# Splitting the down weights and the first row tile's values while the last up products run, in two feed-forward stages of a fused eight-stage network

## What is computed

```python
# L1_ffn: weights (w - zero) * scale, zero and scale per group of 128 rows
gate = jax.nn.silu(jnp.dot(x, gate_proj))
up = jnp.dot(x, up_proj)
return jnp.dot(gate * up, down_proj)
# L3_ffn, the last block: weights w_int * scale, one scale for each matrix
x_mid = jax.nn.silu(x_gate) * x_up
x_out = _qlinear(x_mid, w_down, scale_down)
```

## Time and profile before

| | |
|---|---|
| time, median of 3 runs | 1424.2 us (1423.32 to 1424.61) |
| the profiled execution | 1424.28 us, span 1422.4 us |
| TensorE matmuls busy | 1288.9 us, 91% |
| VectorE busy | 733.9 us, 52% |
| ScalarE busy | 429.2 us, 30% |
| mean granted TensorE clock | 0.949 |
| L376 (up products) in L1 and L3 | 1152 matmuls, 264.4 us |
| L393 (down products) in L1 and L3 | 600 matmuls, 141.7 us |

### The profile page before, as it was taken

One profiled execution on the slowest core, in us unless ns is written; L12 is line 12 of the kernel. 1 busy time (PEld: TensorE's weight loads), 2 busy tenths in 40 slices (PEclk: granted clock), 3 DMA queues, 4 the chain that ended last, 5 costly groups with the idle time before them and its releaser, 6 DMA issues. The chain is left out here.

```text
span 1422.4 us, 14508 instructions
## 1 busy us (share of the span) xinstructions
PE 1288.9 (91%) x5416; PEld 847.6 (60%) x5418; DVE 733.9 (52%) x1283; ACT 429.2 (30%) x718; POOL 162.6 (11%) x211
## 2 busy tenths in 40 slices
PE   7999999699799998983887989989999998799998
PEld 4787666344477787773665434445454443488876
DVE  5322432475666555422756755977776731433264
ACT  2122211211311114210122221156656656221141
POOL 0000000000194100001111250000010124000000
PEclk9999999799899999996889898989999999899999
DMA  8110000830255530003000010000000000112001
GB/s 317 45 44 0 0 0 0 332 148 0 82 202 198 221 139 0 1 23 139 1 1 0 1 45 0 1 1 2 2 2 2 2 3 1 45 67 83 5 23 38
DMA packets 18075, 78.88 MB, mean 55 GB/s; under 512 B 2945, under 2 KB 3585, under 8 KB 15842
## 3 DMA queue, kind: packets, MB, share of 16 engines
q1 hardware_dynamic: 18018, 78.13, 14.9%
HBM read 75.76 MB, written 2.10 MB: 55 GB/s over the span
## 5 line engine op out<-in xcount | busy, mean ns | idle before, releaser
L376 PE MATMUL psum<-L_ffn_x,L_ffn_w_up 128*128 128x512 f32 x1152 | 264.4, 391 | 2.9 <-DVE L_ffn_hidden L505 2.9
L376 PEld LDWEIGHTS psum<-L_ffn_x,L_ffn_w_up 128*128 128x128 f32 x1152 | 217.0, 189 | 50.1 <-DVE L_ffn_hidden L505 4.8
L1814 DVE TENSOR_REDUCE mqa_top<-psum 128x1 f32<-128x512 f32 (+3 forms) x304 | 186.0, 655 | 58.1 <-PE psum L1640 37.7
L1733 ACT ACTIVATE mqa_prob<-psum 128x512 f32<-128x512 f32 x288 | 159.8, 601 | 86.0 <-PE psum L1658 84.9
L393 PE MATMUL psum<-L_ffn_wd,L_ffn_part_h 128*128 128x512 f32 x600 | 141.7, 397 | 7.0 <-DVE L_ffn_wd L301 7.0
L1658 PE MATMUL psum<-mqa_stack,mqa_keys 100*128 100x512 f32 x288 | 133.0, 476 | 4.8 <-DMA mqa_stack<-mqa_rows 3.5
L393 PEld LDWEIGHTS psum<-L_ffn_wd,L_ffn_part_h 128*128 128x128 f32 x600 | 114.3, 192 | 31.7 <-DVE L_ffn_part_h L292 7.8
L1629 PE MATMUL psum<-mqa_keys,mqa_stack 96*128 96x512 f32 (+1 forms) x256 | 108.3, 445 | 1.9 <-DVE mqa_top L1814 1.0
L376 PE MATMUL psum<-L_attn_x,L_attn_w_up 128*128 128x512 f32 x456 | 105.4, 394 | 3.9 <-DVE L_attn_hidden L505 3.9
L376 PEld LDWEIGHTS psum<-L_attn_x,L_attn_w_up 128*128 128x128 f32 x456 | 86.7, 190 | 22.5 <-issue 4.3
L1658 PEld LDWEIGHTS psum<-mqa_stack,mqa_keys 100*128 100x128 f32 x288 | 55.3, 196 | 72.0 <-ACT mqa_prob L1733 62.6
(11 more groups left out here) (246 smaller groups left out, 1698.2 us busy)
## 6 DMA issues: line engine op xcount, KB each, us to landing
L_ffn_stage<-in_L_w SPq DMA_DIRECT2D x25, 768.0 KB, 6.3
L_ffn_z_int<-in_L_z SPq DMA_DIRECT2D x14, 768.0 KB, 4.4
L_ffn_s_all<-in_L_s SPq DMA_DIRECT2D x14, 768.0 KB, 6.2
lora_wo<-in_L_wo SPq DMA_DIRECT2D x8, 1024.0 KB, 8.7
L_attn_stage<-in_L_w SPq DMA_DIRECT2D x10, 512.0 KB, 3.7
L_attn_w_down<-in_L_down SPq DMA_DIRECT2D x1, 2560.0 KB, 24.3
x_feat<-in_x_feat SPq DMA_DIRECT2D x2, 1024.0 KB, 7.0
x_tok<-in_x_tok SPq DMA_DIRECT2D x1, 2048.0 KB, 18.7
```

The costliest lines, as they stand in the source:

```text
L376: ins = nc.tensor.matmul(bank[half][:, :], w_up[:, slot, w_part, at:at + P], x[:, x_part, k, half * HALF:(half + 1) * HALF], start=k == 0 ...
L1733: nc.scalar.activation(prob[:, n % PROBS, :], score_bank[n % 3], ACT.Exp, scale=SCALE)\
L1814: nc.vector.tensor_reduce(top[:, i % 2, lo // HALF, heads[0]:heads[-1] + 1], max_bank[n % 3][:, 0:len(heads) * width] .rearrange("p (h k) ...
```

## The change

Stage L0 keeps its code (`early == 0`). In L3 all down weights (`early = tiles`), and in L1 four of the fourteen (`early = 4`), are split while up products still run.

- **L3.** `wd` moves to memory of its own, and `w_down` shrinks to two slots. In each tile, VectorE now makes the float down weights ahead of the up weights, behind a wait for its own earlier splits; ScalarE casts `wd(0, f)` behind the silu of tile f, and VectorE makes `wd(1, f)` behind its multiplications.
- **L1.** `wd` is made of four pieces that lie where the up phase's buffers end: two tiles in the place of the zeros and scales (free once the last tile's weights are made), two in w_up's slot 0 (free once tile 12's products are done), then eight in x and two in slot 1 (free once all up products are done). The first four are split while tile 13's products run, the other ten behind them.
- **Both.** The last tile's silu and product are taken one half at a time. Behind half 0, both groups' values of row tile 0 are split; row tiles 0 to 3 lie in half 0. The other splits come behind half 1.

The diff, cut:

```diff
+        if zeros is not None:
+            assert (tiles - 1) % 2 == 1
+            part_h = sb("part_h", [P, 2, 2, per, P], F32R)
+            in_front = (front_size - part_size) // (2 * DIM)
+            in_x, in_slot = 2 * KC * TOK // (2 * DIM), 2 * up_width // (2 * DIM)
...
+            places = ([wd_front[:, i, :, :] for i in range(in_front)]
+                      + [wd_slots[:, i, :, :] for i in range(in_slot)]
+                      + [wd_x[:, i, :, :] for i in range(in_x)]
+                      + [wd_slots[:, in_slot + i, :, :] for i in range(in_slot)])
+            early = in_front + in_slot
...
+        elif quantised:
+            early = tiles
...
-        def split_w_down(engine, g, part):
-            for f in groups[g]:
-                if part == 0:
-                    nc.scalar.copy(wd[:, 0, f, :], w_down[:, f, :]).then_inc(wd_hi, 1)
-                else:
-                    engine.wait_ge(wd_hi, base["wd_hi"] + f + 1)
-                    nc.vector.tensor_tensor(wd[:, 1, f, :], w_down[:, f, :], wd[:, 0, f, :].bitcast(F32),
-                                            ALU.subtract).then_inc(wd_lo, 1)
+        def split_w_down(engine, f, part, slot=None):
+            src = w_down[:, f if slot is None else slot, :]
+            if part == 0:
+                nc.scalar.copy(wd(0, f), src).then_inc(wd_hi, 1)
+            else:
+                engine.wait_ge(wd_hi, base["wd_hi"] + f + 1)
+                nc.vector.tensor_tensor(wd(1, f), src, wd(0, f).bitcast(F32),
+                                        ALU.subtract).then_inc(wd_lo, 1)
...
                 def tile(f, slot, first):
                     silu(f, first and slot == 0)
+                    if early == tiles:
+                        split_w_down(act, f, 0, slot)
                     split_w_up(f + 2, slot, False)
...
+                    act.wait_ge(w_lo, base["w_lo"] + tiles)
+                    if early == tiles:
+                        for f in range(tiles - 2, tiles):
+                            split_w_down(act, f, 0, f % 2)
+                    else:
+                        for f in range(in_front):
+                            split_w_down(act, f, 0)
+                        act.wait_ge(up_done, base["up_done"] + 2 * tiles - 2)
+                        for f in range(in_front, early):
+                            split_w_down(act, f, 0)
+                    silu(tiles - 1, halves=(0,))
+                    act.wait_ge(product, base["product"] + 2 * tiles - 1)
+                    for g in range(2):
+                        split_h(act, 0, g, 0)
+                    silu(tiles - 1, halves=(1,))
+                    act.wait_ge(up_done, base["up_done"] + 2 * tiles)
+                    for f in range(early, tiles):
+                        split_w_down(act, f, 0)
+                    act.wait_ge(product, base["product"] + 2 * tiles)
...
                     elif quantised:
                         dve.wait_ge(loaded[slot], base["loaded"][slot] + 8 * (f - slot) + 16)
+                        if not first:
+                            dve.wait_ge(wd_lo, base["wd_lo"] + f - 1)
+                        nc.vector.tensor_scalar(w_down[:, slot, :], w_int[:, slot, up_width:width], sc[:, 2:3], None,
+                                                ALU.mult)
...
-                multiply(tiles - 1)
-                for g in range(2):
-                    split_h(dve, 0, g, 1)
-                    split_w_down(dve, g, 1)
+                if early == 0:
...
+                else:
+                    for f in range(tiles - 2 if early == tiles else 0, early):
+                        split_w_down(dve, f, 1, f % 2 if early == tiles else None)
+                    multiply(tiles - 1, halves=(0,))
+                    for g in range(2):
+                        split_h(dve, 0, g, 1)
+                    multiply(tiles - 1, halves=(1,))
+                    for f in range(early, tiles):
+                        split_w_down(dve, f, 1)
```

More of the change, by code:

```diff
@@ L418, in split_w_up, with silu @@
                     nc.scalar.copy(w_up[:, slot, 0, :], stage[:, slot, 0:up_width]).then_inc(w_hi, 1)
-                def silu(f, fresh=False):
-                    for half in range(2):
+                def silu(f, fresh=False, halves=(0, 1)):
+                    for half in halves:
                         act.wait_ge(gate_done, base["gate_done"] + 2 * f + half + 1)
@@ L438, in _ @@
                 silu(tiles - 2)
-                silu(tiles - 1)
-                act.wait_ge(product, base["product"] + 2 * tiles)
-                if not quantised:
+                if early == 0:
+                    silu(tiles - 1)
+                    act.wait_ge(product, base["product"] + 2 * tiles)
                     act.wait_ge(down_loaded, 16)
+                    for g in range(2):
+                        split_h(act, 0, g, 0)
+                        for f in groups[g]:
+                            split_w_down(act, f, 0)
[4 more added lines that the diff above has]
+                            split_w_down(act, f, 0, f % 2)
+                    else:
+                        for f in range(in_front):
[6 more added lines that the diff above has]
+                    for g in range(2):
+                        split_h(act, 0, g, 0)
+                    silu(tiles - 1, halves=(1,))
+                    act.wait_ge(up_done, base["up_done"] + 2 * tiles)
+                    for f in range(early, tiles):
+                        split_w_down(act, f, 0)
+                    act.wait_ge(product, base["product"] + 2 * tiles)
                 if table is not None:
                     act.wait_ge(table.half_ready, 1)
-                for g in range(2):
-                    split_h(act, 0, g, 0)
-                    split_w_down(act, g, 0)
                 split_h(act, 1, 0, 0)
@@ L492, in split_w_up @@
                         ins.then_inc(dequantised, 1)
-                        nc.vector.tensor_scalar(w_down[:, f, :], w_int[:, slot, up_width:width], sc[:, 2:3], None,
-                                                ALU.mult)
                     if first and slot == 0:
@@ L499, in split_w_up, with multiply @@
                                             w_up[:, slot, 0, :].bitcast(F32), ALU.subtract).then_inc(w_lo, 1)
-                def multiply(f):
-                    for half in range(2):
+                def multiply(f, halves=(0, 1)):
+                    for half in halves:
                         dve.wait_ge(gated, base["gated"] + 2 * f + half + 1)
@@ L509, in tile @@
                     multiply(f)
+                    if early == tiles:
+                        split_w_down(dve, f, 1, slot)
                     split_w_up(f + 2, slot, False)
@@ L518, in _ @@
                 multiply(tiles - 2)
-                multiply(tiles - 1)
-                for g in range(2):
-                    split_h(dve, 0, g, 1)
-                    split_w_down(dve, g, 1)
+                if early == 0:
+                    multiply(tiles - 1)
+                    for g in range(2):
+                        split_h(dve, 0, g, 1)
+                        for f in groups[g]:
+                            split_w_down(dve, f, 1)
+                else:
+                    for f in range(tiles - 2 if early == tiles else 0, early):
+                        split_w_down(dve, f, 1, f % 2 if early == tiles else None)
+                    multiply(tiles - 1, halves=(0,))
+                    for g in range(2):
+                        split_h(dve, 0, g, 1)
+                    multiply(tiles - 1, halves=(1,))
+                    for f in range(early, tiles):
+                        split_w_down(dve, f, 1)
                 split_h(dve, 1, 0, 1)
```

29 lines of the change are left out of this document (23 added, 6 removed).

## The result

| | before | changed |
|---|---|---|
| median | 1424.05 us (1421.98 to 1424.61, 6 runs) | 1414.93 us (1412.49 to 1417.74, 6 runs) |
| profiled execution | 1424.28 us, span 1422.4 | 1412.49 us, span 1410.5 |
| ratio | | 0.9939, 95% interval 0.9927 to 0.995 |

The change makes the kernel 9.1 us faster by the medians, and the interval of the ratio (7.1 to 10.4 us) is clear of zero. A second series on another chip gave the changed kernel 1414.23 us and before 1422.69, ratio 0.9937 (0.9924 to 0.9951).

A forecast was written before the change was run, and what follows sets the result against it. TensorE was taken to bound the kernel except in the holes; gains of 5.4 us in L1 and 5.16 in L3, together 10.56 off 1424.28, gave 1413.7 us, range 1411.4 to 1416.8 (8 in 10: 1411.2 to 1417.4).

The forecast's parts named there:

- The holes: TensorE's idle time ahead of the down products, 3.64 us in L1 and 3.40 in L3, would close to 0 to 0.3.
- T: The end of L1's last up product, put at 539.87 us, from which the readiness of weights and values was counted.
- The falls of the clock: Behind each hole in L1 and L3, TensorE's slow stretch would go, worth 1.6 us each.
- the drops stay: Rival: in L1 and L3 only the holes close and the clock still falls, giving 1416.9 us; chance 0.11.
- L3's loop: The work added to each L3 tile lengthens VectorE's chain from 3.82 to 5.0 us but costs nothing.
- The slower outcome: Rival: the added work in L3's loop makes up weights late, 1.5 us a tile, ending slower; chance 0.03.
- The next stage: The stage behind L1 starts once L1's last row tile is done, so L1's 5.4 us is handed on.
- Matmuls reading `wd` from other places are the same matmuls: Moving the down weights' buffer was taken to leave the down products unchanged, at no cost.
- the term for L3: L3's forecast gain: 3.40 idle, 0.16 lost at the hole and 1.6 of slow clock, 5.16 us.
- The allowance: 2 us to either side for run spread and the clock in stages behind L1, widening 1413.4 to 1414.8.

The follow-up runs named there:

- e7_fill4: The kernel before, with four useless float32 products added behind the last up product in L1 and in L3; 1421.21 us, ratio 0.9979.
- e1_l1_only: The changed kernel with stage L3 run as before, so only L1 is changed; 1418.91 us, ratio 0.9959.
- e2_l3_only: The changed kernel with stage L1 run as before, so only L3 is changed; 1420.55 us, ratio 0.9976.
- e6_pause: The changed kernel, with L3's down products made to wait for the stage's last product; 1416.31 us, ratio 0.9939.
- e8_parts: The changed kernel, but no weight split early in L1 and L3's values split behind the last product; 1420.72 us, ratio 0.9975.

## Why the prediction was right, and its one wrong step

The forecast was 1413.7 us and the median is 1414.93. The mechanism is the forecast one, point by point, but for one step:

- **The holes** close in both stages, as worked out: no idle time at the first down product. L1's values end at 538.15 for 538.4 forecast, 0.12 us of which is that all of L1 lies earlier in this execution (last multiplication at 539.79 for 539.91). Its fifth weight is ready at 541.07, 1.39 us behind the end of the last up product at 539.68, for T + 1.4. (The prediction put T at 539.87; by the earlier trace rows it is 543.44 - 3.64 = 539.80. No sum of it hangs on these 0.07 us.)
- **The falls of the clock** go with them. This was a reading of the trace before; `e7_fill4` shows it apart from all else, 3.0 us (1.7 to 4.3) for 3.2. Of the rivals, "the drops stay" is out. The size of a fall, 1.6 us, is that of one execution; `e1_l1_only` had one that cost 0.9 us more. How often the unprofiled runs of the kernel before had their falls, no row tells.
- **L3's loop** costs nothing. One tile of the changed kernel, VectorE's chain from product to product:

```profile
1245.82 0.69 DVE L564 TENSOR_TENSOR L_ffn_hidden<-L_ffn_gate,psum 128x512 f32<-128x512 f32 x1 [4.75 <-PE psum L411]
1246.43 0.68 DVE L336 TENSOR_TENSOR L_ffn_wd<-L_ffn_w_down,L_ffn_wd 128x512 fp32r<-128x512 f32 x1
1247.22 0.49 DVE L547 TENSOR_SCALAR L_ffn_w_down<-L_ffn_stage,L_ffn_sc 128x512 f32<-128x512 int32 x1
...
1249.62 1.23 DVE L557 TENSOR_TENSOR L_ffn_w_up<-L_ffn_stage,L_ffn_w_up 128x1024 fp32r<-128x1024 f32 x1 [1.12 <-ACT L_ffn_w_up L453]
...
1251.37 0.69 DVE L564 TENSOR_TENSOR L_ffn_hidden<-L_ffn_gate,psum 128x512 f32 x1 [0.53 <-PE psum L411]
```

  It is 1249.62 + 1.23 - 1245.82 = 5.03 us long (5.0 forecast; 3.82 in the earlier trace rows), and VectorE still idles 0.53 us ahead of the next product (0.5 forecast). The 504 up products take 114.25 us, as in the earlier trace rows. The slower outcome is out by a wide margin.
- **The next stage** hands L1's gain on: 5.6 us at its first transfer (5.4 forecast).
- **The wrong step** is the sentence "Matmuls reading `wd` from other places are the same matmuls". They are not. In L3 they stood 0.0067 us wider apart, 1.76 us in all, and the term for L3 is 3.5 in place of 5.16. With it the sum is 5.4 + 3.4 = 8.8, against 9.1 measured. I costed the move of a buffer at nothing, and the trace before could show no price: every stretch that I had read as 0.227 had its operands a multiple of 512 bytes apart, which a profile, without addresses, doesn't tell. The verdict on the time doesn't hang on it: 1.76 us more is 1415.5, inside the range.
- **The allowance** of 2 us for other stages' clock was needed: the median lies 0.1 us above the 1413.4 to 1414.8 that the prediction gave for one execution without it, and the changed kernel's runs spread over 5.3 us, before's over 2.6.

## What to carry to other kernels

A hole between two phases on the engine that bounds the kernel costs its length and then what the clock loses behind it; here holes of 3.4 and 3.6 us cost 5.2 and 5.4, and in one execution 0.9 us more. Look which links of the chain behind the last result depend on that result at all (here one of four), and move the others under the phase before, in memory that has come free by then. When a change moves an operand of a matmul to other memory, count matmuls in an equal stretch before and after, and if they differ, try the buffer at a multiple of 256 bytes from the other operand. Here that was worth 1.7 us in the trace, too little for the timed runs to confirm.

## What the runs showed of the hardware that I had not expected

- For L3's down products (128x512 matmuls in the rounded float32 type, each with its own weights, at clock 1.00), the spacing is 0.2267 us when the two operands' starts are a multiple of 256 bytes apart, and 0.2289 (64 bytes) or 0.2333 (32 and 128 bytes) when they are not. Of the changed kernel only the moving operand was shifted to try this.
- At all four idle times of 3.40 and 3.64 us (L1 and L3 before, L3 in `e1_l1_only`, L1 in `e2_l3_only`) TensorE fell to half clock, once already while it waited and otherwise 0.2 to 1.4 us behind its next matmul, with mean clocks from 0.76 to 0.60 over the next 7 us. At idle times of 0.85, 1.54 and 2.71 us (`e6_pause`, `e8_parts`) it did not, in one profile each.
- A float32 product of 128x512 is two instructions 0.43 us apart, and filling each of two holes with four of them made the kernel 3.0 us faster (1.7 to 4.3).
